# Content of the score stacks sent ahead of the cosine exchange, with two half-buffers each for sines and cosines

## The reference

```
q, k, v = heads(xn @ Wq.T + bq), heads(xn @ Wk.T + bk), heads(xn @ Wv.T + bv)   # 16 heads of 8
r = pos_emb(256)                                   # [sin | cos], 256 x 8
rel = einsum('bhqd,ld->bhql', q + u, r)
scores = (einsum('bhqd,bhkd->bhqk', q, k) + rel_shift(rel)) * 8 ** -0.5
p = softmax(where(future, NEG, scores))
```

## Time and profile before

| | us |
|---|---|
| median of 3 runs | 2379.78 |
| lowest and highest of them | 2377.61, 2389.59 |
| time of the profiled execution | 2385.99 |
| its span, first to last instruction | 2384.0 |

### The profile page before, as it was taken

One profiled execution on the slowest core, in us unless ns is written; L12 is line 12 of the kernel. 1 busy time (PEld: TensorE's weight loads), 2 busy tenths in 40 slices (PEclk: granted clock), 3 DMA queues, 4 the chain that ended last, 5 costly groups with the idle time before them and its releaser, 6 DMA issues. The chain is left out here.

```text
span 2384.0 us, 83086 instructions
## 1 busy us (share of the span) xinstructions
PE 2283.0 (96%) x31360; PEld 1975.4 (83%) x31360; DVE 2007.8 (84%) x4943; ACT 1838.8 (77%) x2869; POOL 1140.9 (48%) x2089
## 2 busy tenths in 40 slices
PE   4899999999999999999999999999999999799998
PEld 3788888888888888888888888888888888677776
DVE  5799999988888888888888888888888885677774
ACT  2588888888888888888888888888888888555554
POOL 4455555554555555545555555455554443333332
PEclk8899999999999999999999999999999999899999
DMA  5444433333333333333333333333343331000000
GB/s 125 107 109 111 107 91 93 92 87 92 86 86 96 91 93 93 87 92 84 90 91 96 93 92 86 92 86 87 92 110 90 88 93 37 21 28 28 27 23 19
DMA packets 227432, 196.04 MB, mean 82 GB/s; under 512 B 29025, under 2 KB 225761, under 8 KB 227041
## 3 DMA queue, kind: packets, MB, share of 16 engines
q1 hardware_dynamic: 227040, 190.73, 30.5%
HBM read 14.46 MB, written 4.19 MB: 8 GB/s over the span
## 5 line engine op out<-in xcount | busy, mean ns | idle before, releaser
L995 DVE TENSOR_REDUCE rowmax<-bank 128x4 f32<-128x1024 f32 (+1 forms) x768 | 916.1, 1220 | 104.4 <-PE bank L572 72.2
L813 ACT ACTIVATE probs<-bank 128x1024 f32<-128x1024 f32 x768 | 738.3, 1024 | 77.3 <-PE bank L632 76.8
L572 PE MATMUL bank<-kstack,qstack 62*128 62x256 f32 (+1 forms) x4096 | 417.5, 301 | 8.1 <-DMA qstack<-base 8.1
L632 PE MATMUL bank<-qstack,kstack 64*128 64x128 f32 (+1 forms) x4096 | 424.1, 299 | 0.0
L854 ACT ACT_TABLE_LOAD x256 | 328.4, 1283 | 4.5
L572 PEld LDWEIGHTS bank<-kstack,qstack 62*128 62x128 f32 x4096 | 316.7, 193 | 8.5 <-issue 8.5
L632 PEld LDWEIGHTS bank<-qstack,kstack 64*128 64x128 f32 x4096 | 316.5, 192 | 0.0
L1169 POOL CAST xn1T_parts<-xn1T 128x256 fp32r<-128x256 f32 x128 | 50.7, 396 | 491.8 <-ACT xn1T L821 491.8
L594 PE MATMUL bank<-maskT_half,pick_half 64*128 64x128 bf16 (+1 forms) x3072 | 267.9, 241 | 15.3 <-DVE turn_c L964 5.8
L534 PE MATMUL bank<-mask_half,pick_half 64*128 64x128 bf16 (+1 forms) x3072 | 268.6, 243 | 9.4 <-DVE h_all L1030 4.1
L721 PE MATMUL bank<-w,hidden 128*128 128x128 f32 x2048 | 273.5, 277 | 2.7 <-ACT hidden L863 2.7
(11 more groups left out here) (153 smaller groups left out, 5298.2 us busy)
## 6 DMA issues: line engine op xcount, KB each, us to landing
qstack<-base SPq DMA_DIRECT2D x768, 128.0 KB, 2.4
kstack<-base SPq DMA_DIRECT2D x384, 128.0 KB, 2.5
turn_x<-turn_c SPq DMA_DIRECT2D x512, 32.0 KB, 1.8
qstack<-maxrows SPq DMA_DIRECT2D x256, 16.0 KB
out<-ot SPq DMA_DIRECT2D x16, 256.0 KB, 2.4
h_all<-in_x SPq DMA_DIRECT2D x7, 512.0 KB, 5.4
xin<-in_x SPq DMA_DIRECT2D x14, 256.0 KB, 3.1
w<-in_w SPq DMA_DIRECT2D x8, 256.0 KB, 3.4
```

What stands on the lines that cost most here:

```text
L572: last = pe.matmul(bank[:, b0 + b, i * wide:(i + 1) * wide], qstack[rows, r, p0 + i, t * 128:(t + 1) * 128], kstack[rows, r, p0 + i, 0:wid ...
L632: last = pe.matmul(bank[:, b0 + b, i * wide:(i + 1) * wide], kstack[rows, r, p0 + i, kt * 128:(kt + 1) * 128], qstack[rows, r, p0 + i, q0: ...
L813: act.activation(probs[:, k], bank[:, A_BANK[k]:A_BANK[k] + 2, :], ACT.Exp, scale=SCALE).then_inc(exp_done[k], 1)
L995: dve.tensor_reduce(rowmax[:, n % 2, t, :, p0:p0 + heads], bank[:, M_BANK[k]:M_BANK[k] + 2, :].rearrange("p b (h c) -> p b h c", h=heads), ...
```

## The change

It has four parts. On SyncE, `content` runs for tile s in slot s, ahead of `exchange(s)`; it ran for tile s-1 in slot s, which was behind it. `turned_content` and `maxima` follow the exchange and the loads of their slot. On GpSimd, `turned(s-1)` runs in slot s behind `xn2_split(s-6)`, where `turned(s)` ran at the end of slot s. `turn_s` and `turn_c` have two halves that tiles use in turn, and the waits before their writing go back one tile further.

```diff
-        turn_s = sb("turn_s", [128, S])
-        turn_c = sb("turn_c", [128, S])
+        turn_s = sb("turn_s", [128, 2, S])
+        turn_c = sb("turn_c", [128, 2, S])
...
-                    sp.dma_start(turn_x[32 * c:32 * c + 32], turn_c[o:o + 32]).then_inc(turn_landed, 16)
+                    sp.dma_start(turn_x[32 * c:32 * c + 32], turn_c[o:o + 32, n % 2]).then_inc(turn_landed, 16)
...
                 if live(s - 1):
-                    content(s - 1)
-                if live(s - 1):
                     turned_content(s - 1)
                 if live(s - 3):
                     maxima(s - 3)
+                if live(s):
+                    content(s)
                 if live(s):
                     exchange(s)
...
-                at_least(dve, turn_landed, 64 * n)
-                dve.scalar_tensor_tensor(turn_c[:], bank[:, QK_BANK, 0:S], b_cols[:, layer(n), 2:3], turn[:, 1],
+                at_least(dve, turn_landed, 64 * (n - 1))
+                dve.scalar_tensor_tensor(turn_c[:, n % 2], bank[:, QK_BANK, 0:S], b_cols[:, layer(n), 2:3], turn[:, 1],
...
-                at_least(dve, rot_ready, n)
+                at_least(dve, rot_ready, n - 1)
...
-                pool.tensor_tensor(rotated[:], turn_s[:], turn_x[:], ALU.add).then_inc(rot_ready, 1)
+                pool.tensor_tensor(rotated[:], turn_s[:, n % 2], turn_x[:], ALU.add).then_inc(rot_ready, 1)
...
                 if live(s - 6):
                     xn2_split(s - 6)
+                if live(s - 1):
+                    turned(s - 1)
...
-                if live(s):
-                    turned(s)
```

More of the change, by code:

```diff
@@ L968, in turn_sines @@
                 dve.wait_ge(qk_first, n + 1)
-                at_least(dve, rot_ready, n)
-                dve.scalar_tensor_tensor(turn_s[:], bank[:, QK_BANK, 0:S], b_cols[:, layer(n), 2:3], turn[:, 0],
+                at_least(dve, rot_ready, n - 1)
+                dve.scalar_tensor_tensor(turn_s[:, n % 2], bank[:, QK_BANK, 0:S], b_cols[:, layer(n), 2:3], turn[:, 0],
                                          ALU.add, ALU.mult).then_inc(sines_used, 1)
```

## The result

| | before | after |
|---|---|---|
| median of 6 runs each, same chip, us | 2381.52 | 2368.55 |
| lowest and highest | 2377.12, 2389.59 | 2363.42, 2369.99 |
| profiled execution | 2385.99 | 2369.68 |
| its span | 2384.0 | 2367.7 |

A forecast was written before the change was run, and what follows sets the result against it. TensorE, 96% busy, was taken to bound the kernel. Start 6.6, loads 3.9 and boundaries 2.4 sum to 12.9 us, less 0.5 for hiccups 12.4, giving 2367.4 us; range 2361 to 2383.

The forecast's parts named there:

- Start: First tiles of the pipeline: less waiting for content and maxima behind loads, and a higher clock; gain 6.6 us, bounds 0 and 8.
- T(0): Rotated content of the first tile, which TensorE waits for at the pipeline's start: lands some 3.3 us later.
- M(0): Maxima of the first tile, at the pipeline's start: late behind b_o and w_o, landing at some 57.3; gain 1.5 us.
- M(2): Maxima of tile 2, at the start: issued at 86 to 87 behind loads, landing at about 88.8; gain 5.3 us, 1.5 included.
- the prediction's own sign: At the start, TensorE's wait at 92.88 should be under 1.5 us, with the clock full behind it.
- Loads: Loaded tiles after the start: content no longer lands late behind loads; gain 3.9 us, bounds 2 and 4.8.
- Boundaries: Layer boundaries: waits for xn2T_parts go, 4.2 us, less 1.8 for late maxima in three tiles; gain 2.4 us.
- The steady tile: Tiles of the steady stretch stay at 15.33 us: later rotated content and maxima cost 0, covered by 1.0 to 1.6 us slack.
- The hiccups: Exchanges that take longer, like 2.86 us after 2.46, of which a few use up the maxima's slack: 0.5 us taken off.
- The start gives nothing: Rival, pipeline start: rotated content and maxima are as late behind loads as content was; 3.3 us left, 2376.5; chance 0.19.
- The turned chain sets the tile: Rival, steady tiles: content, exchange, rotation, rotated content, maxima in sequence decide the length; 0.5 us per tile, 2428; chance 0.12.
- Hidden waits: Rival, steady stretch: TensorE's busy time hides waits; tile 13.5 us, kernel 220 us faster, 2160; chance 0.02.

The follow-up runs named there:

- e3_sync_only: The kernel before with SyncE's order alone changed to content, exchange, loads, rotated content, maxima: 2445.35 us, ratio 1.0252 to the kernel before.

## Why the prediction was right

**The sum.** On the profiled executions it was 12.4 us; it came out as 16.3. By the medians the change gave 13.0, by the ratio 15, and in its second measurement 18.2. 2368.55 is inside the range, and the sign of each term was right. That it lies only 1.2 us from the forecast of 2367.4 is in part luck: the traces gained 2.7 us more than the sum up to tile 127, and the gain of the same kernel differs by 3 to 5 us between measurements. One end of the range does not follow from its rule: half way between the lower bounds and the forecast is 2371.8 and not 2374; the result lies inside either.

**Start: 6.6 us forecast, 7.9 measured.** The steps in order, the first tiles of the change beside the earlier trace rows:

```profile
29.50 0.80 PE L572 MATMUL bank<-kstack,qstack 62*128 62x256 f32 x4 [6.74 <-DMA qstack<-base]
...
51.18 0.84 ACT L836 ACTIVATE base<-bank,b_cols 128x256 fp32r<-128x256 f32 x2 [7.81 <-PE bank L127]
...
55.30 0.28 PE L594 MATMUL bank<-maskT_half,pick_half 64*128 64x256 bf16 x2 [2.10 <-DVE turn_c L964]
...
56.01 0.33 PE L632 MATMUL bank<-qstack,kstack 64*128 64x128 f32 x2 [0.42 <-DMA qstack<-maxrows]
...
88.09 0.33 PE L632 MATMUL bank<-qstack,kstack 64*128 64x128 f32 x2 [2.51 <-DMA qstack<-maxrows]
...
96.30 0.36 PE L125 MATMUL bank<-xn1T_parts,w_now 128*128 128x256 f32 x1
```

T(0) came 3.0 us later (3.3 forecast). The split of tile 3 started at 51.18 and was released by TensorE's product (51.9, by the same releaser). The masks started at 55.30 (56.2). M(0) was mis-sized: forecast at 57.3 behind w_o, which took 7.8 us to land in the kernel before. Here w_o is issued at 48.66 and lands 3.9 us later, ahead of M(0), whose second transfer starts near 53.9; the group ran at 56.01, late by only 0.42 us. TensorE then came to the group of tile 5 at 85.6 and not 87.8, so what M(0) gave was spent in waiting there, and M(2) set the start:

```profile
84.00 1.17 SPq L468 DMA_DIRECT2D qstack<-maxrows  x2
```

M(2) was issued at 84.00, where 86 to 87 was forecast, but took 3.5 us to the matmul at 88.09 (88.8 forecast), behind a load of 512 KB. So TensorE idled 2.51 us, where the forecast asked for less than 1 to gain the clock, and the prediction's own sign for less than 1.5. The clock stayed up all the same in this trace, and from 88.09 to 96.30 are 8.2 us where the same stretch took 10.1. This is luck in part. In the second trace of the change TensorE waited 2.09 us for M(2), until 86.89, and the clock fell behind it:

```profile
88.00:92.00 4.00, 3.84 (x28) 2.68 (x24) 3.69 (x12) 3.29 (x5) 0.80 (x2) 0.57 0.51 139
```

The same stretch then took 8.6 us (86.89 to 95.50), and the start still gained 8.7 us. So less than 1 us of idle time was not needed in the first trace, and the length of this one wait doesn't tell the two traces apart. Of the 1.3 us that the start gained above its terms, 0.7 lie at the start of the group of tile 5 (88.09 and not 88.8) and 0.6 in the stretch behind it (8.2 us, where 8.75 was taken from the steady tile).

**Loads: 3.9 forecast, 4.9 measured** (2.6 and 2.3). At the experts' loads TensorE's two visible waits were 2.4 us and 2.3 went, so the 0.5 us taken back there was not needed. At the loads of x three waits of 2.05 us were counted and 2.6 us went; 0.28 of the rest is a fourth wait, ahead of 235.67, that the sum left out.

**Boundaries: 2.4 forecast, 2.3 measured**, and by the forecast's road: the waits for xn2T_parts went, and M came late in their place. The third boundary of the changed kernel:

```profile
1576.11 0.33 PE L632 MATMUL bank<-qstack,kstack 64*128 64x128 f32 x2 [1.11 <-DMA qstack<-maxrows]
...
1586.55 2.94 SPq L460 DMA_DIRECT2D qstack<-base  x3
...
1592.29 0.33 PE L632 MATMUL bank<-qstack,kstack 64*128 64x128 f32 x2 [0.71 <-DMA qstack<-maxrows]
```

Forecast were 0.3 to 0.9 us for M in three tiles. It was 0.18 and 0.27 us at the first two boundaries (593.39 and 1084.25). At the third it is 1.11 us, and 0.71 one tile later, each behind a T whose issue took 2.81 and 2.94 us instead of 1.86. Together they are 2.3 us, where 1.8 were forecast.

**The steady tile: 0 forecast, 0 measured**, with the slack of M at 1.5 us. The hiccups, for which 0.5 us was taken off, exist; in the steady tiles they cost nothing that the marks tell, and at the third boundary two long issues of T stand ahead of the late M.

**Behind tile 127** the sum had no term, and 1.2 us were gained. It is within what two traces of the change differ by there (2.6 us), and goes with the granted clock, as the section on the result says.

**The rivals.** *The start gives nothing* is excluded by 7.9 us. *The turned chain sets the tile* did not happen, but its mechanism is real. M's landing was 2.0 us in steady tiles and not the 3.4 that this rival needs (behind a load it was 3.5, in tile 5). Delayed by 1.32 us it costs 36 us; and with the rotation where it was, the late exchange costs 62. What keeps it away is GpSimd's order and some 1.5 us on SyncE; that e3_sync_only was expected to gain shows that I had taken a landing level with its reader for one in time. *Hidden waits*: the tile stayed at 15.31 us, so nothing in TensorE's 99% was freed, and no run was made to test it. The Trainium skill ("Perfetto Trace Analysis", Identifying the Most-Contended Engine) judges by the work done against the peak and by the weight loads' share, and 435.95 of 500 us of weight loads still leave it possible; no run here shows it.

**What the blind sum did not say** is which edit it pays for. Its largest terms come from content ahead of the loads, which needs one line moved in SyncE's order. The swap with the exchange costs 3 us at the first rotated content, of which 0.5 to 2.2 are left by tile 6, and the halves do nothing.

## What to carry to other kernels

In a queue that one engine issues in order, ask of each entry what stands ahead of it that nobody waits for soon: moving long loads behind short transfers that release a busy engine gave, alone, as much as the whole change, and changing the order among the short ones was not needed. Look at the landing and not only at the issue: the loads took 0.4 to 0.6 us each to issue, and what stood behind them landed up to 5.7 us late. When a producer is moved later, look for who waits for it in order on another engine and what is queued behind that wait; the same move cost 62 us with one order there and with another only 2 to 3 us at the start. Slack worked out from one tile does not hold for all: delay the transfer by a known amount on purpose, and the run shows its landing and in how many tiles the slack is less.

## What the runs showed of the hardware

- The same program can keep its clock or lose it at the same place. In the change's first trace TensorE idled 2.51 us ahead of 88.09, and the granted clock was 1.00 from 85 to 97 us, all at 2.4 GHz. In its second trace it idled 2.09 us ahead of 86.89, and the clock was 0.57 in 88 to 92 us, most of it at 1.2 GHz. Before, 4.12 us ahead of 92.88 were followed by 0.60 in 93 to 97. The length of that one idle time doesn't tell what the clock does.
- A transfer of 16 KB between two places on the chip landed within 2.0 us of its issue in steady tiles, one of 32 KB in 1.9 and one of 128 KB in 2.5: an eighth of the bytes saves a fifth of the time.
- Behind loads from memory in the same queue these times grow: 128 KB took 7.1 and 8.1 us in the kernel before (issues at 48.98 and 82.86) and 2.4 with the loads behind them; 16 KB took 3.5 us behind a load of 512 KB (issue at 84.6 in the change).
- SyncE needs about 0.6 us to issue one transfer of these, and in 57 of 78 tiles of the change at least one group of issues took 0.3 to 1.6 us more.
